# Attention of a two-layer recurrence: context as the stationary operand, or context streamed through column tiles of TensorE

## The reference, cut to what matters

```python
def step(carry, x_t):
    h0, c0, h1, c1, a = carry
    xin = jnp.concatenate([x_t, a], axis=-1)
    h0, c0 = _lstm_cell(xin, h0, c0, Wi0, Wh0, bi0, bh0)
    h1, c1 = _lstm_cell(h0, h1, c1, Wi1, Wh1, bi1, bh1)
    q = h1 @ Wq.T
    attn = jax.nn.softmax(jnp.einsum('bh,bsh->bs', q, context), axis=-1)
    mixed = jnp.einsum('bs,bsh->bh', attn, context)
    a2 = jnp.tanh(jnp.concatenate([mixed, h1], axis=-1) @ Wo.T + bo)
    return ((h0, c0, h1, c1, a2), a2)
_, outs = jax.lax.scan(step, carry0, jnp.swapaxes(inputs, 0, 1))
```

## Time and profile before

| what | value |
|---|---|
| median of 3 runs | 1902.4 us (1902.16 to 1904.66) |
| the profiled execution | 1905.45 us, span of its instructions 1903.7 us |
| TensorE matmul busy | 1474.6 us (77%) |
| TensorE weight load busy | 1281.8 us (67%) |
| VectorE busy | 1184.7 us (62%) |
| ScalarE busy | 761.3 us (40%) |
| recurrence, first to last tanh of group a | 615.3 to 1511.1 us |

### The profile page before, as it was taken

One profiled execution on the slowest core, in us unless ns is written; L12 is line 12 of the kernel. 1 busy time (PEld: TensorE's weight loads), 2 busy tenths in 40 slices (PEclk: granted clock), 3 DMA queues, 4 the chain that ended last, 5 costly groups with the idle time before them and its releaser, 6 DMA issues. The chain is left out here.

```text
span 1903.7 us, 82660 instructions
## 1 busy us (share of the span) xinstructions
PE 1474.6 (77%) x34335; PEld 1281.8 (67%) x34336; DVE 1184.7 (62%) x4397; ACT 761.3 (40%) x1849; POOL 209.3 (11%) x427
## 2 busy tenths in 40 slices
PE   1547777777734999999999999999999874039997
PEld 0446666666613888888888888888888763026665
DVE  5878888888785665666566566566656575014444
ACT  2446566656564343343344334334333311013332
POOL 0000000000001000000000000000000001743333
PEclk9778888899856999999999999999999855569999
DMA  6000000000034000000000000000000070222222
GB/s 210 1 2 0 0 0 0 0 0 0 1 89 201 2 0 0 0 0 0 0 0 0 0 0 0 0 0 0 0 0 0 4 229 20 103 80 72 71 71 51
DMA packets 42813, 57.39 MB, mean 30 GB/s; under 512 B 5754, under 2 KB 32892, under 8 KB 40856
## 3 DMA queue, kind: packets, MB, share of 16 engines
q1 hardware_dynamic: 36672, 42.90, 7.5%
q0 software_dynamic: 5376, 12.66, 1.9%
q10 hardware_dynamic: 728, 1.34, 0.2%
HBM read 30.52 MB, written 26.88 MB: 30 GB/s over the span
## 5 line engine op out<-in xcount | busy, mean ns | idle before, releaser
L1518 DVE TENSOR_TENSOR hb<-psH,b_sb 128x512 f32<-128x512 f32 x72 | 49.8, 692 | 168.9 <-issue 89.2
L900 PE MATMUL sc_a<-h_a,KH 128*128 128x32 f16 (+1 forms) x4096 | 122.7, 176 | 2.5 <-DVE h_a L1058 2.5
L940 PEld LDWEIGHTS mx_a<-pmv_a,VH 128*128 128x128 f16 x4096 | 106.8, 96 | 25.0 <-DVE pmv_a L1087 24.7
L940 PE MATMUL mx_a<-pmv_a,VH 128*128 128x32 f16 (+1 forms) x4096 | 112.8, 176 | 13.8 <-DVE pmv_a L1087 13.6
L940 PEld LDWEIGHTS mx_b<-pmv_b,VH 128*128 128x128 f16 x4096 | 106.7, 96 | 24.9 <-DVE pmv_b L1087 24.9
L940 PE MATMUL mx_b<-pmv_b,VH 128*128 128x32 f16 (+1 forms) x4096 | 112.6, 176 | 13.8 <-DVE pmv_b L1087 13.8
L900 PE MATMUL sc_b<-h_b,KH 128*128 128x32 f16 (+1 forms) x4096 | 121.7, 176 | 0.0
L860 PE MATMUL z_a<-h_a,WL 128*128 128x64 f16 x2304 | 112.7, 194 | 9.6 <-DVE h_a L1050 1.9
L860 PE MATMUL z_b<-h_b,WL 128*128 128x64 f16 x2304 | 112.4, 193 | 9.5 <-issue 1.1
L900 PEld LDWEIGHTS sc_a<-h_a,KH 128*128 128x128 f16 x4096 | 112.0, 96 | 2.7 <-DVE h_a L1058 2.6
L462 PE MATMUL psK<-ident,xn 128*128 128x128 f32 x64 | 21.6, 338 | 117.7 <-DVE VB L667 91.1
(11 more groups left out here) (282 smaller groups left out, 3775.1 us busy)
## 6 DMA issues: line engine op xcount, KB each, us to landing
sorted_x<-zt SPq DMA_DIRECT2D x9, 1032.0 KB, 11.9
xr<-sorted_x SPq DMA_DIRECT2D x72, 65.0 KB
xg<-sorted_x SPq DMA_DIRECT2D x72, 64.0 KB
XT<-in_ctxT SPq DMA_DIRECT2D x1, 4096.0 KB, 13.1
x_scratch<-X SPq DMA_DIRECT2D x1, 4096.0 KB, 15.9
TOK<-x_scratch SPq DMA_DIRECT2D x4, 1024.0 KB, 9.9
w_sb<-in_w SPq DMA_DIRECT2D x1, 2048.0 KB, 12.8
b_sb<-in_b SPq DMA_DIRECT2D x1, 2048.0 KB, 20.1
```

The lines of the kernel that those rows point to most:

```text
L900: mm = nc.tensor.matmul(A.S[:, WIDE * n:WIDE * n + streamed(n)], KH[:, k, pair * P:(pair + 1) * P], A.h[1][:, 2 * n:2 * n + streamed(n) // ...
L940: mm = nc.tensor.matmul(A.M[:, WIDE * n:WIDE * n + streamed(n)], VH[:, k, pair, :], A.pm[:, n, 0:streamed(n)], start=False, stop=False, sk ...
L1518: nc.vector.tensor_tensor(hb[:, u, :], psH[:, u, :], b1_sb[:, bass.ds(col, FF)], ALU.add).then_inc(v_hb, 1)
```

## The change: what it does

The roles in the two large products are turned. The context now streams, and h1 and p are the weights. A weight block is 128 rows by 32 columns, of which one column (h1) or two (p) hold data and the others are zeros. h1 is written by VectorE into `hw`, 32 columns for each sequence, always at column 15; a matmul reads 32 adjacent columns, shifted so that the data column comes to the place of its sequence. The results of 32 sequences so add up in one 32-partition strip of PSUM: rows are batches.

Each such matmul works on one of four column tiles of the array. `scores` issues 16 rounds of 2 parts of 4 tiles for the high part of h1 (128 matmuls, 64 columns of `KH` streamed each) and 16 rounds of 4 for the low part (64 matmuls; low times low is no longer computed). They are issued as two blocks, before and behind the gates of `L`. `mixing` uses 64-row by 32-column tiles, eight at a time, with 128 columns of `VH` streamed: 128 matmuls.

The mask, line 917's pair and the placing of p go away. The maximum is taken over 128 partitions (two strips hold the even, two the odd sequences), a second VectorE instruction subtracts it and scales (`d`), and exp follows. p is transposed by two f32 matmuls against `dg`, a diagonal with 1/sum in it. The mixing leaves rows in two PSUM banks, which VectorE and ScalarE copy to `mr`, and two f32 matmuls against `fold` bring them back to columns and add them to Wo times h1 in `q.out`. GpSimd makes a contiguous copy `h1` for the gates. `hidden_low(1)` now stands behind VectorE's copy of the mixing, and `early0x` behind the mixing. The zeroing of the wide tiles moves to the stage before; `zt` is half as large and is sent 18 times.

```diff
@@ -22,10 +22,12 @@
 GP = GB // 2
 NE, FF = 8, 512
 FC = FF // P
-WIDE = 512 // GP
-STREAM = 2 * WIDE
-PAD = (STREAM - 4) // 2
-NSPLIT = 24
+QUAD = 32
+NQ = P // QUAD
+HALFQ = QUAD // 2
+EIGHT = QUAD // 4
+H_AT = HALFQ - 1
+P_AT = HALFQ - 2
 S = 4096.0
 NT = B * T // P + NE
@@ -280,24 +273,21 @@
                     nc.vector.tensor_scalar(
...
+                        pick[:, :, :].rearrange("p h (j i) -> p h j i", j=2),
+                        ident[:, :].rearrange("p (h j w) -> p h j w", h=2, j=2)[:, :, :, 0:HALFQ],
+                        S, None, ALU.mult).then_inc(v_b, 1)
+                    nc.vector.tensor_reduce(
+                        fold[:, :].rearrange("p (j i) -> p j i", j=NQ),
+                        ident[:, :].rearrange("p (j i k) -> p j i k", j=NQ, k=2)[:, :, 0:EIGHT, :],
+                        AX.X, ALU.add).then_inc(v_b, 1)
@@ -684,6 +674,9 @@
+hw = [sbr(f"hw_{t}", [P, 2, GB, QUAD], F16) for t in "ab"]
+pw2 = [sbr(f"pmw_{t}", [P, GP, QUAD], F16) for t in "ab"]
@@ -701,12 +694,20 @@
...
+
+@block.gpsimd
+def _(pool):
+    for g in range(2):
+        pool.memset(hw[g][:, :, :, :], 0.0).then_inc(g_win, 1)
+        pool.memset(pw2[g][:, :, :], 0.0).then_inc(g_win, 1)
+    pool.wait_ge(g_win, 4)
...
@@ -779,37 +780,40 @@
...
+    q.h0 = sb(f"h0_{t}", [P, GB, 2], F16)
+    q.hw = hw[g]
+    q.h1 = sb(f"h1_{t}", [P, 2, GB], F16)
...
+    q.nm = sb(f"nm_{t}", [P, 1])
+    q.d = sb(f"d_{t}", [P, T])
+    q.p = sb(f"p_{t}", [P, T])
+    q.sum = sb(f"sum_{t}", [P, 1])
+    q.r = sb(f"r_{t}", [P, 1])
+    q.dg = sb(f"dg_{t}", [P, 2, GP])
+    q.pm = pw2[g]
+    q.mr = sb(f"mr_{t}", [P, 2, D])
...
+    q.pT = q.S[:, T:T + GP]
+    q.rows = [q.M[:, 0:D], q.S[:, P:P + D]]
+    q.out = q.M[:, 2 * P:2 * P + GB]
...
@@ -886,61 +890,77 @@
     def early1(q):
         bias(q, 1)
...
+        gates(q, 1, WH1, [q.h1[:, k, :] for k in range(2)])
+
+    def scores(q, k, parts):
+
+        for i in range(HALFQ):
+            for part in parts:
+                for t in range(NQ):
+                    b = 2 * (HALFQ * (t % 2) + i) + t // 2
+                    at = b * QUAD + H_AT - i
+                    mm = nc.tensor.matmul(q.S[QUAD * t:QUAD * (t + 1), 0:T],
+                                          q.hw[:, k, :, :].rearrange("p b w -> p (b w)")[:, at:at + QUAD],
+                                          KH[:, part, (q.g * GB + b) * T:(q.g * GB + b + 1) * T],
+                                          start=(k == 0 and i == 0 and part == 0),
+                                          stop=(k == 1 and i == HALFQ - 1), skip_group_check=True)
+        return mm
+
+    def mixing(q):
+
+        win = q.pm[:, :, :].rearrange("p n w -> p (n w)")
+        for i in range(EIGHT):
+            for part in range(2):
+                for j in range(NQ):
+                    n = EIGHT * j + i
+                    at = n * QUAD + P_AT - 2 * i
+                    for h in range(2):
+                        mm = nc.tensor.matmul(q.rows[h][QUAD * j:QUAD * (j + 1), :],
+                                              win[T * h:T * (h + 1), at:at + QUAD],
+                                              VH[T * h:T * (h + 1), part, q.g * GP + n, :],
+                                              start=False, stop=False, skip_group_check=True)
+        return mm
     def half(L, A, lt, at):
         last = isinstance(at, int) and at == T - 1
...
+        if A:
+            pe.wait_ge(A.s_h[1], 2 * at + 1)
+            scores(A, 0, (0, 1))
+        if L:
+
+            gates_as_ready(L, 0, WA0, [L.a[:, :, k] for k in range(2)], L.s_ah, lt).then_inc(L.s_z[0], 1)
         if A:
             pe.wait_ge(A.s_h[1], 2 * at + 2)
...
+            scores(A, 1, (0,)).then_inc(A.s_sc, 1)
             if not last:
                 early0h(A)
...
+            pe.wait_ge(A.s_hc, at + 1)
             if not last:
                 early1(A)
         if L:
...
+            gates_as_ready(L, 1, WI1, [L.h0[:, :, k] for k in range(2)], L.s_h[0],
                            lt + 1).then_inc(L.s_z[1], 1)
         if A:
...
+            pe.wait_ge(A.s_dg, at + 1)
+            for h in range(2):
+                mm = nc.tensor.matmul(A.pT[T * h:T * (h + 1), :], A.p[:, :], A.dg[:, h, :],
+                                      start=True, stop=True)
+            mm.then_inc(A.s_pt, 1)
+            for k, (w, m) in enumerate(((0, 0), (1, 0), (0, 1))):
+                if k == 2:
+                    pe.wait_ge(A.s_pm, 2 * at + 2)
+                nc.tensor.matmul(A.out, WO2[:, w, :], A.h1[:, m, :],
+                                 start=(k == 0), stop=False, skip_group_check=True)
+            mixing(A).then_inc(A.s_mx, 1)
             if not last:
                 early0x(A, at + 1)
...
+            pe.wait_ge(A.s_me, at + 1)
+            pe.wait_ge(A.s_mo, at + 1)
+            for h in range(2):
+                mm = nc.tensor.matmul(A.out.rearrange("p (n h) -> p n h", h=2)[:, :, h], A.mr[:, h, :],
+                                      fold[:, :], start=False, stop=False, skip_group_check=True)
+            mm.then_inc(A.s_ar, 1)
     for q in G:
         early0h(q)
@@ -970,17 +990,19 @@
             out_gate(0)
             cell_tanh(0)
         if A:
...
+            act.wait_ge(A.s_d, at + 1)
+            nc.scalar.activation(A.p[:, :], A.d[:, :], ACT.Exp,
                                  accum_out=A.sum[:, 0:1]).then_inc(A.s_ex, 1)
         if L:
             gate_tanh(1)
             out_gate(1)
             cell_tanh(1)
         if A:
+            act.wait_ge(A.s_mx, at + 1)
+            nc.scalar.activation(A.mr[:, 1, :], A.rows[1], ACT.Copy).then_inc(A.s_mo, 1)
             act.wait_ge(A.s_ar, at + 1)
             wait(act, A.s_ao, at)
...
+            nc.scalar.activation(A.a32[:, :], A.out, ACT.Tanh, bias=bo_sb[:, 0:1],
                                  scale=sc[:, IV:IV + 1]).then_inc(A.s_ta, 1)
     run_halves(half, act)
@@ -990,24 +1012,26 @@
     pool.wait_ge(v_zt, 1)
     pool.memset(zt[:, :, AT_ROW:].bitcast(I32), NOWHERE).then_inc(v_zt, 1)
     for q in G:
...
+        for tile in (q.h0, q.h1, q.a):
             pool.memset(tile[:, :, :], 0.0).then_inc(s_zero, 1)
         for tile in (q.c[0], q.c[1]):
             pool.memset(tile[:, :], 0.0).then_inc(s_zero, 1)
         for k in range(2):
             pool.tensor_copy(q.xs[:, k, :], XT[:, k, 0, q.g * GB:(q.g + 1) * GB]).then_inc(s_zero, 1)
...
+    pool.wait_ge(s_zero, 14)
     for q in G:
         pool.sem_inc(q.s_xs, 1)
     def half(L, A, lt, at):
+        if A:
+            pool.wait_ge(A.s_h[1], 2 * at + 2)
         if L:
             if not (isinstance(lt, int) and lt == T - 1):
                 pool.wait_ge(L.s_xu, lt + 1)
                 pool.tensor_copy(L.xs[:, :, :], XTn(L, lt + 1)).then_inc(L.s_xs, 1)
         if A:
+            pool.tensor_copy(A.h1[:, :, :], A.hw[:, :, :, H_AT]).then_inc(A.s_hc, 1)
             pool.wait_ge(A.s_ta, at + 1)
             pool.tensor_copy(X[:, bass.ds(at * B + A.g * GB, GB)], A.a32[:, :]).then_inc(A.s_ao, 1)
@@ -1055,46 +1082,39 @@
         def hidden_low(l):
             dve.wait_ge(L.s_h32[l], lt + 1)
             dve.wait_ge(L.s_h[l], 2 * lt + 1)
...
+            nc.vector.tensor_tensor(part(l, 1), L.h32[l][:, :], part(l, 0),
                                     ALU.subtract).then_inc(L.s_h[l], 1)
...
         if L:
             cell(0)
         if A:
...
+            dve.wait_ge(A.s_sc, at + 1)
+            nc.vector.tensor_reduce(A.nm[:, :], A.S[:, 0:T], AX.X, ALU.max,
                                     negate=True).then_inc(A.s_nm, 1)
+            dve.wait_ge(A.s_nm, at + 1)
+            nc.vector.tensor_scalar(A.d[:, :], A.S[:, 0:T], A.nm[:, 0:1], sc[:, IK:IK + 1],
+                                    ALU.add, ALU.mult).then_inc(A.s_d, 1)
         if L:
             hidden(0)
+            hidden_low(0)
         if A:
             dve.wait_ge(A.s_ex, at + 1)
             nc.vector.reciprocal(A.r[:, :], A.sum[:, :]).then_inc(A.s_r, 1)
...
             dve.wait_ge(A.s_r, at + 1)
...
+            nc.vector.tensor_scalar(A.dg[:, :, :], pick[:, :, :], A.r[:, 0:1], None,
+                                    ALU.mult).then_inc(A.s_dg, 1)
             dve.wait_ge(A.s_pt, at + 1)
...
+            nc.vector.tensor_copy(A.pm[:, :, P_AT], A.pT).then_inc(A.s_pm, 1)
             dve.wait_ge(A.s_pm, 2 * at + 1)
...
+            nc.vector.tensor_tensor(A.pm[:, :, P_AT + 1], A.pT, A.pm[:, :, P_AT],
                                     ALU.subtract).then_inc(A.s_pm, 1)
         if L:
             cell(1)
...
             hidden(1)
...
         if A:
             dve.wait_ge(A.s_mx, at + 1)
...
+            nc.vector.tensor_copy(A.mr[:, 0, :], A.rows[0]).then_inc(A.s_me, 1)
+        if L:
+            hidden_low(1)
         if A:
             dve.wait_ge(A.s_ta, at + 1)
             nc.vector.tensor_scalar(A.a[:, :, 0], A.a32[:, :], S, None, ALU.mult).then_inc(A.s_ah, 1)
```

(35 more changed lines are left out.)

103 lines of the change are left out of this document (16 added, 87 removed).

## The result

The changed kernel takes **2497.4 us** (median of 4 runs, 2488.4 to 2509.6), the kernel before 1902.3 on the same chip: a ratio of 1.313, 95% interval 1.307 to 1.319. I had forecast 1923 and a range up to 1985. The sign is right, the size is not: +595 us instead of +20.

A forecast was written before the change was run, and what follows sets the result against it. TensorE was taken to bound the half. 128 halves going from 7.11 to 7.30 us gave +24, savings ahead of the loop -4, so +20 over the kernel before: 1923 us, range 1865 to 1985.

The forecast's parts named there:

- rival E: Outside the half: the loop's doubled code is fetched again, or the clock falls to 1.2 GHz; above 2200 us; 5%.
- Mechanism A: Half as summed: scores behind the folds, not tanh, release the gates, later by 0.25; half 7.30 us, total 1923; 43%.
- From the zero to the mixing: From the gates' last start through maximum, `d`, exp and p's transposition: mixing starts at 3.90 us, before at 3.87.
- Mixing: TensorE's 16 rounds of eight tiles, 0.056 us a round: 0.90 us instead of 1.66, stream ending at 4.80.
- D: Sequencer can't feed the small tiles: 4.4 ns an instruction, rounds of 0.035 and 0.070, 0.38 us a half, 1972 us; 13%.
- Copies: Behind the mixing: both copies from 5.00 to 5.29 us, folds from 5.34, last fold starting at 5.73.
- Scores: First scores behind the folds: 32 rounds, 0.96 us, from 5.92 to 6.88, with the change of tile back 6.97.
- Changes of tile: TensorE's switches of tile shape: 0.09 us each, three on the path (into mixing, into and out of first scores).
- rival B: Faster: tile changes between two f16 shapes cost nothing; half 7.03 us, total 1888 us; 34%.
- C: Small tiles go no faster than full ones beyond a burst: 25.4 ns a matmul, +5.2 us a half, 2590 us; 5%.
- my -3.6: Ahead of the loop: half of `zt` and the zeroings of `pmv`, h and `pe` go away, saving 3.6 us.
- GpSimd's copy of h1: Copy takes about 0.35 us, done before 7.3, hidden because `early1` comes 1.1 us into the next half; 0.9 to spare.

The follow-up runs named there:

- the doubled kernel before: Kernel before with TensorE's loop turn of two steps instead of one, same matmuls and order: 2125.9 us, ratio 1.117; with back edge announced 1905.2 us.
- the run between: Changed kernel without VH's low part in column tiles 2 and 3, back edge not announced, 1478 TensorE instructions a turn: 1996.0 us, ratio 1.049.

## Why the prediction was wrong

**The step that failed is the choice in rival E**: "its code doubles (some 1600 TensorE instructions a turn, before 830) and has to be fetched again", which I gave 5%. It carries 470 of the 595 us. I had the count and not the price: "above 2200 us" was worked out for the clock's fall alone. The trace of before showed only that a turn of 830 is kept: its last fetch of code ahead of the loop's end lies at 637.6 us, when the loop had just begun. No row spoke for one of 1600. The Trainium skill (Runtime: NRT & Kernel Launch, section Instruction fetch mechanics) gives TensorE room for 2048 instructions, refilled in blocks of 256. That a turn of 1606 would therefore stay was my inference, not the page's. The 16 KB fetches and the stops at every 256 instructions agree with its blocks. Its size is not refuted either: a turn of 1606 touches eight blocks, which are just 2048 instructions, and stays when the back edge is announced. What failed is that a turn smaller than the room stays without that. I had no reason beyond that room to put E at 5%.

**The clean half: 7.85 to 7.89 us, not 7.30.** Mechanism A is right in its order: in the half above the scores follow the folds, the high part of `a` is ready at 900.88 - 0.04 = 900.84 (7.10), and TensorE turns to it at 7.51: the scores are last, by 0.41 where I had 0.25. With half of them moved away, `a` is. But its terms are too small by 0.55:

- From the zero to the mixing: the first matmul at 4.08, I said 3.90. The maximum and `d` start a little early (1.27, 1.53), but `d` takes 0.34 instead of 0.24, `dg` 0.25 instead of 0.21 and ends at 2.84 instead of 2.73, and p's transposition starts at 2.90, not 2.78. The third WO2 is at 3.94, not 3.78. Sum 0.18.
- Mixing: 1.04 us from first to last start, where my rounds make 0.85. Of that 0.15 is D: 8.2 ns a matmul instead of 7.0; the rest is that I let a round's matmuls start at once. Sum 0.20.
- Copies start at 5.40 and the folds at 5.82, the last fold at 6.15, where I had 5.00, 5.34 and 5.73: the handovers take longer, the folds a little less. Sum 0.04.
- Scores: 6.35 to 7.38 by their starts, the gates at 7.51, where I had 5.92 and 6.97. The 128 and the change take 1.03 and 0.13; I had 0.96 and 0.09. Sum 0.11, most of it D again. The change ahead of them and the gates behind them add 0.02.

So D, which I gave 13% as a case of its own, is true in its effect and worth about 0.22 us a half; I had said 0.38. Behind its first eight matmuls a block of scores keeps near the pace of the columns up to about the fortieth, 7.3 ns a start, and the mixing up to about the 24th, 7.0 ns; after that both go at 8.33, that is 4.17 ns for each of the two instructions of a matmul. Line 449's burst of 32, my evidence, is too short to show this, as I wrote under D without giving it weight. VectorE's terms were read off neighbours of another shape: `d` works on 128 partitions with two operands per partition. The trace of before has three lines that do the same (617, 748 and 1452), with 128 columns instead of 64; their 0.34 to 0.36 us would have been a closer bound than the 0.24 I took:

```profile
L1452 DVE TENSOR_SCALAR TOK<-TOK,mvc,rsc 128x128 f32<-128x128 f32 x64 | 16.8, 347 | 0.1
```

**Changes of tile: right.** Between two f16 shapes they take 0.120 to 0.133 us from start to start, also in the clean half (893.74 to 893.86), so 0.09 to 0.10 above the 0.030 of a gate. A's price holds, and rival B, which had 34%, is false.

**C: false.** Starts are 8 ns apart, not 25, over streams of 128. So the trace did not agree with the rule of the Trainium skill that I had weighed, and line 449 was right to speak against it.

**Outside of the loop.** From the zeroing of `zt` to the first bias matmul pass 3.1 us, before 6.1: -3.0 of my -3.6. The wide zeroings lie at 528 to 537 us beside other work, as said. GpSimd's copy of h1 ends later than I said, at 7.89 and not before 7.3, for it stands behind the copy of the last tanh; `early1` wants it 1.2 us into the next half, so it stays hidden. But the unrolled halves ahead of the loop and behind it are new code too, fetched while TensorE works through it: with the announced loop the first tanhs are 11.3, 13.7 and 12.3 us apart (before, the first 8.5), and the last two 12.7 and 9.6. I had no term for it.

**The sum.** With the loop announced the span is 2026.6, 122.9 us over the 1903.7 of before. Some 124 halves in the loop by 0.76 are 94; the rest of 29 is what the unrolled halves at both ends cost, with the 3.0 saved and a us or two by which the stages ahead differ from run to run. My +20 had 0.19 where the half lost 0.76, nothing for the ends, and nothing of the 470.

## What to carry to other kernels

Count the instructions of a loop's turn on the engine that bounds it, before and after, and treat a turn that grows past what the trace has shown to be kept as the first risk, not the last: here a turn that grew from 824 to some 1606 instructions cost 470 us by its fetches and the low clock that they brought, nearly four times the 125 us of everything else. If the profile's instruction queue has packets inside a loop, announce the back edge or shorten the turn before judging anything else. When a rate is read from a burst, ask how long the burst is: in this kernel a small tile costs 8.33 ns with its load once a block is longer than some 24 to 40 matmuls, and taking half of the columns from half of them changed nothing.

## What the runs showed that I had not expected

- A fetched turn costs not the transfer (16 KB each) but its turnaround: one block of 256 instructions per 3.7 us, and 3.8 to 4.8 us for the branch. TensorE uses up a block of small tiles in about 1.1 us.
- The changed kernel (1606 a turn) is fetched again in every second turn, but for two places; the doubled kernel before (1643) in every one. Both touch eight blocks; no run tells why they differ.
- Announcing the back edge removes all fetches in a loop whose turn is not kept without it: 470 us here, 221 in the doubled kernel. Why it does so for a turn of this length, when without it the same turn is fetched block after block, stays open.
- Writing h1 at a stride of 64 bytes (one of 32 f16 columns) costs VectorE 0.45 us where the write of h0 by the same line, at a stride of 4 bytes, takes 0.22. It is off the path: h1 is there at 5.09 us and wanted at 6.35.
- Leaving out work can lower the clock: without VH's low part it falls to the 1.2 GHz level in some halves and 1350 instructions a turn give 8.35 us there, while with the 1478 of the run between it stays at 1.00 and all take 7.67. Why it falls in just those halves is not shown.
